# The lead of self and cross attention: four maxima products side by side in PSUM and one reduction for the four

## What is computed

```python
h1 = _ln(x, n1_g, n1_b)
x = _attn(h1, h1, q1, k1, v1, o1_w, o1_b, heads) + x        # self, 20 heads of 16, 512 keys
h2 = _ln(x, n2_g, n2_b)
x = _attn(h2, context, q2, k2, v2, o2_w, o2_b, heads) + x   # cross, 20 heads of 16, 1024 keys
...
sim = jnp.einsum('bhid,bhjd->bhij', q, k) * scale
a = jax.nn.softmax(sim, axis=-1)
```

## Time and profile before

| | us |
|---|---|
| median of three runs | 925.62 |
| the profiled execution | 928.74 |
| its span, first to last instruction | 926.9 |
| TensorE busy in the span | 851.4 |
| VectorE busy in the span | 615.8 |
| ScalarE busy in the span | 470.8 |
| mean granted TensorE clock | 0.936 of full speed |

### The profile page before, as it was taken

How to read it: one execution, slowest core, us unless ns; L and a number is a source line. 1 busy time by engine, 2 the same in 40 slices (tenths; PEclk the granted TensorE clock), 3 DMA queues, 4 the chain that set the end, 5 groups by cost and what they waited for, 6 DMA issues and landing times.

```text
span 926.9 us, 11358 instructions
## 1 busy us (share of the span) xinstructions
PE 851.4 (92%) x4148; PEld 465.4 (50%) x4148; DVE 615.8 (66%) x1156; ACT 470.8 (51%) x682; POOL 82.1 (9%) x109
## 2 busy tenths in 40 slices
PE   4769989999999999999999789999999999799998
PEld 3646744444466576333334433333333332478988
DVE  4245547777683555799966587899999991756132
ACT  4523444445552441466675403667777679465030
POOL 3200000400004021000000300000000000130000
PEclk9977999999997998599999955999999999989999
DMA  6938668632302065122216230222222000600000
GB/s 219 273 113 238 195 179 261 179 97 85 101 19 65 0 197 175 48 68 68 62 28 111 74 108 1 53 53 53 53 52 53 1 2 2 240 1 1 29 1 29
DMA packets 30966, 83.18 MB, mean 90 GB/s; under 512 B 5172, under 2 KB 9212, under 8 KB 28606
## 3 DMA queue, kind: packets, MB, share of 16 engines
q1 hardware_dynamic: 30110, 79.71, 30.4%
q0 software_dynamic: 800, 2.73, 1.0%
HBM read 56.12 MB, written 25.89 MB: 88 GB/s over the span
## 4 chain that ended last, share of the span: by engine, by line
PE 60%; DVE 25%; DMA 7%; ACT 4%; issue 3%; POOL 1%; SPq 0%; DVEq 0%; ACTq 0%; POOLq 0%
PE PS L859 16%; PE PS L802 13%; DVE maxp L961 10%; PE PS L1390 8%; PE PS L553 8%; PE PS L839 6%; DVE negm L961 5%; PE PS L1402 4%; DMA k_d<-split 2%; DMA q_sl<-msplit 2%; PE PS L1200 2%; DMA ca_nat<-in_ca 2%; DVE turned L994 1%; ACT probs L925 1%; DVE stats L1243 1%
## 5 line engine op out<-in xcount | busy, mean ns | idle before, releaser
L925 ACT ACTIVATE probs<-PS 128x1024 f32<-128x1024 f32 (+1 forms) x336 | 311.7, 971 | 153.0 <-PE PS L839 147.4
L961 DVE TENSOR_REDUCE maxp<-PS 128x1 f32<-128x512 f32 x448 | 280.1, 679 | 49.9 <-PE PS L802 48.9
L802 PE MATMUL PS<-k_sl,q_sl 48*128 48x512 f32 (+3 forms) x640 | 264.1, 493 | 23.5 <-DMA q_sl<-q_d 11.1
L802 PEld LDWEIGHTS PS<-k_sl,q_sl 48*128 48x128 f32 (+2 forms) x640 | 120.2, 201 | 201.1 <-DVE maxp L961 121.2
L839 PE MATMUL PS<-q_sl,k_sl 50*128 50x512 f32 (+3 forms) x672 | 204.2, 434 | 9.4 <-ACT probs L925 5.2
L961 DVE TENSOR_REDUCE negm<-PS 128x1 f32<-128x512 f32 (+1 forms) x192 | 120.9, 679 | 28.1 <-PE PS L802 28.0
L839 PEld LDWEIGHTS PS<-q_sl,k_sl 50*128 50x128 f32 (+2 forms) x672 | 103.3, 192 | 57.2 <-ACT probs L925 24.6
L859 PE MATMUL PS<-probs,v2c 128*32 128x512 f32 x640 | 88.3, 622 | 1.0
L591 DVE TENSOR_TENSOR split<-PS,split 128x512 fp32r<-128x512 f32 (+3 forms) x54 | 34.9, 650 | 48.7 <-ACT split L568 48.5
L859 PE MATMUL PS<-probs,v0c 128*64 128x512 f32 (+1 forms) x256 | 62.9, 612 | 0.0
L568 ACT CAST split<-PS 128x512 fp32r<-128x512 f32 (+3 forms) x54 | 29.9, 553 | 56.0 <-PE PS L553 46.5
(11 more groups left out here) (180 smaller groups left out, 1005.4 us busy)
## 6 DMA issues: line engine op xcount, KB each, us to landing
k_d<-split SPq DMA_DIRECT2D x20, 512.0 KB, 3.5
q_d<-split SPq DMA_DIRECT2D x12, 512.0 KB, 3.2
k_sl<-k_d SPq DMA_DIRECT2D x8, 640.0 KB
k_sl<-k_d SPq DMA_DIRECT2D x40, 128.0 KB
q_sl<-q_d SPq DMA_DIRECT2D x40, 128.0 KB
k_sl<-k_d SPq DMA_DIRECT2D x20, 256.0 KB
w_raw<-in_ff_w SPq DMA_DIRECT2D x1, 3840.0 KB, 11.7
k_d<-split SPq DMA_DIRECT2D x10, 256.0 KB, 3.7
```

Of the source, the lines that this page charges most:

```text
L802: nc.tensor.matmul(PS[0:a.qt, SBANKS[k % 3], 0:cn], q_view(g)[f:f + a.rows, j // a.stack, q * a.qt:(q + 1) * a.qt], k_view(g)[f:f + a.rows ...
L925: nc.scalar.activation(probs[0:a.size[t], x % PRING, :, 0:a.nq], PS[0:a.size[t], 2 * (x % 2):2 * (x % 2) + 2, 0:a.nq], ACT.Exp, scale=a.sc ...
L961: nc.vector.tensor_reduce((maxp if nch > 1 else negm)[0:a.qt, g.turn, o:o + 1], PS[0:a.qt, SBANKS[k % 3], 0:a.chunks[c][1]], AX.X, ALU.max ...
```

## The change

In a stream whose first group has `stack` 2 (self and cross attention) the lead is written anew; the steps behind it and the first block's attentions stay.

- TensorE (`wide_items`): the four items of chunk c go to four neighbouring banks, 0 to 3 for even c and 4 to 7 for odd c. From chunk 2 on TensorE waits, once for each chunk, until the chunk that had these banks is reduced.
- VectorE (`wide_maxima`): one reduction reads the four banks, 128 x 2048 elements, and writes four columns. It waits for all four items and adds 4 to `score_free` at its end.
- The flip in the lead takes the last bank of the set that the next chunk uses (`flip_bank`). It waits until the chunk ahead of its own is reduced, and the next chunk's fourth item waits for ScalarE's copy of it.
- Behind the lead TensorE waits until all chunks but the last are reduced, since the first scores go to banks 0 to 3.

```diff
+    def wide_bank(c):
+
+        return 4 * (c % 2)
+
+    def flip_bank(st, i):
+
+        at_chunk = st.first_step[i + 1] if i + 1 < len(st.groups) else len(st.steps)
+        if st.groups[0].a.stack == 2 and at_chunk < st.lead:
+            return wide_bank(at_chunk + 1) + 3
+        return SBANKS[st.flip_use[i] % 3]
+
     def pe_attention(pe, st, side=None):
+        wide = st.groups[0].a.stack == 2
+
+        def wide_items(c):
+            per = st.groups[0].a.per_step
+            if c >= 2:
+                pe.wait_ge(st.score_free, per * (c - 1))
+            for n, (i, m) in enumerate(st.chunk(c)[1]):
...
+                if n == 3 and c and st.chunk(c - 1)[0] is not None:
+                    pe.wait_ge(st.flipped, st.chunk(c - 1)[0] + 1)
+                c0, cn = a.chunks[part]
+                f = a.base(j)
+                nc.tensor.matmul(PS[0:a.qt, wide_bank(c) + n, 0:cn],
...
+                                 start=True, stop=True).then_inc(st.score, 1)
+            if st.chunk(c)[0] is not None:
+                pe.wait_ge(st.score_free, per * c)
+                flip(st.chunk(c)[0], waits=False)
...
         for x in range(st.lead):
-            maxima([x])
...
-            flips([x])
+            if wide:
+                wide_items(x)
...
+        if wide:
+            pe.wait_ge(st.score_free, st.groups[0].a.per_step * (st.lead - 1 + st.lead % 2))
...
+        def wide_maxima(c):
+            ended, items = st.chunk(c)
+            if ended is not None:
+                part_maxima(ended)
...
+            dve.wait_ge(st.score, st.item_at[i, m] + a.per_step)
...
+            nc.vector.tensor_reduce(to, PS[0:a.qt, wide_bank(c):wide_bank(c) + 4, :].rearrange(
+                "p (c e) n -> p c e n", e=a.stack), AX.X, ALU.max,
+                negate=len(a.chunks) == 1).then_inc(st.score_free, a.per_step)
```

More of the change, by code:

```diff
@@ L784, in sp_cross @@
                 sp_load(sp, st, i + SLOTS)
-    def pe_attention(pe, st, side=None):
+    def wide_bank(c):
[5 more added lines that the diff above has]
+        return SBANKS[st.flip_use[i] % 3]
+    def pe_attention(pe, st, side=None):
+        wide = st.groups[0].a.stack == 2
[4 more added lines that the diff above has]
+            for n, (i, m) in enumerate(st.chunk(c)[1]):
+                g = st.groups[i]
+                a = g.a
+                j, q, part = a.items[m]
+                if m == 0:
+                    pe.wait_ge(q_loaded[g.place], g.loads)
+                if n == 3 and c and st.chunk(c - 1)[0] is not None:
[3 more added lines that the diff above has]
+                nc.tensor.matmul(PS[0:a.qt, wide_bank(c) + n, 0:cn],
+                                 q_view(g)[f:f + a.rows, j // a.stack, q * a.qt:(q + 1) * a.qt],
+                                 k_view(g)[f:f + a.rows, j // a.stack, c0:c0 + cn],
+                                 start=True, stop=True).then_inc(st.score, 1)
+            if st.chunk(c)[0] is not None:
+                pe.wait_ge(st.score_free, per * c)
+                flip(st.chunk(c)[0], waits=False)
         def bank_free(k):
@@ L805, in item, with flip @@
                              start=True, stop=True).then_inc(st.score, 1)
-        def flip(i):
+        def flip(i, waits=True):
             g = st.groups[i]
             a = g.a
-            k = st.flip_use[i]
             pe.wait_ge(st.m_low, i + 1)
-            bank_free(k)
-            nc.tensor.transpose(PS[0:2 * a.cols, SBANKS[k % 3], 0:a.qt],
+            if waits:
+                bank_free(st.flip_use[i])
+            nc.tensor.transpose(PS[0:2 * a.cols, flip_bank(st, i), 0:a.qt],
                                 mparts[0:a.qt, g.turn, 0:2 * a.cols].bitcast(F32),
@@ L865, in pe_attention @@
         for x in range(st.lead):
-            maxima([x])
-            if side is not None:
-                pe_projection(pe, side, share(side, x, st.lead))
-            flips([x])
+            if wide:
+                wide_items(x)
+            else:
+                maxima([x])
+                if side is not None:
+                    pe_projection(pe, side, share(side, x, st.lead))
+                flips([x])
+        if wide:
+            pe.wait_ge(st.score_free, st.groups[0].a.per_step * (st.lead - 1 + st.lead % 2))
         if side is not None:
@@ L909, in flipped @@
                     nc.scalar.copy(msplit[0:2 * a.cols, g.turn, 0:a.qt],
-                                   PS[0:2 * a.cols, SBANKS[st.flip_use[i] % 3], 0:a.qt]).then_inc(st.flipped, 1)
+                                   PS[0:2 * a.cols, flip_bank(st, i), 0:a.qt]).then_inc(st.flipped, 1)
         for c in range(st.lead):
@@ L963, in reduce @@
                                     AX.X, ALU.max, negate=nch == 1).then_inc(st.score_free, 1)
+        def wide_maxima(c):
+            ended, items = st.chunk(c)
+            if ended is not None:
+                part_maxima(ended)
+            i, m = items[0]
+            g = st.groups[i]
+            a = g.a
+            t = m // a.per_step
+            dve.wait_ge(st.score, st.item_at[i, m] + a.per_step)
+            if len(a.chunks) > 1:
+                to = maxp[0:a.qt, g.turn, :].rearrange("p (e r c) -> p r c e", e=a.stack, c=2)[:, t, :, :]
+            else:
+                to = negm[0:a.qt, g.turn, :].rearrange("p (e r c) -> p r c e", e=a.stack, c=2)[:, t, :, :]
+            nc.vector.tensor_reduce(to, PS[0:a.qt, wide_bank(c):wide_bank(c) + 4, :].rearrange(
+                "p (c e) n -> p c e n", e=a.stack), AX.X, ALU.max,
+                negate=len(a.chunks) == 1).then_inc(st.score_free, a.per_step)
         def maxima(chunks, normalising=None):
@@ L1008, in dve_attention @@
         for x in range(st.lead):
-            maxima([x])
-            if side is not None:
-                dve_projection(dve, side, share(side, x, st.lead))
+            if st.groups[0].a.stack == 2:
+                wide_maxima(x)
+            else:
+                maxima([x])
+                if side is not None:
+                    dve_projection(dve, side, share(side, x, st.lead))
         for s, (i, t) in enumerate(st.steps):
```

## The result

| | before | changed |
|---|---|---|
| median of 22 runs each, us | 927.6 | 924.0 |
| lowest and highest | 922.9, 932.4 | 915.1, 933.1 |
| the profiled execution, us | 928.7 | 915.5 |
| self lead, first item to first scores, us | 18.9 | 16.8 |
| cross lead | 28.7 | 25.8 |

The account below looks back on a forecast made before the run. VectorE was taken to bound both leads. First chunk, wide reductions at 2.17 us, `part_maxima` and hand-over gave 16.5 and 25.8 us, saving 2.4 + 2.8 = 5.2 us: 925.6 - 5.2 = 920.4 us, range 916.0 to 925.5.

Parts of the forecast that it names:

- What bounds the leads: Both attention leads: VectorE's reductions, 0.599 us apart, set the pace and TensorE waits for its banks.
- The pitch, P = 2.17 us: Leads: wide reductions of 2.25 us, overlapping by 0.08 us, start 2.17 us apart; four single ones take 2.40 us.
- The fear that crossing a bank costs something: Rival, wide reductions in the leads: bank or segment costs raise the pitch to 2.40 us; gain 1.1 us, 924.5 us; chance 0.12.
- First chunk: Start of each lead: VectorE waits for four items instead of starting after 0.50 us; 0.73 us self, 1.2 us cross.
- Middle and end of the lead: `part_maxima` takes 0.34 and 0.55 us, flip hidden; first scores wait until 2.2 us of VectorE work remains, not 1.9.
- The sum for the leads: First item to first scores: 16.5 us self, 25.8 us cross; gains of 2.4 and 2.8 us, together 5.2 us.
- The items hide: Leads: TensorE refills four banks in some 1.2 us during a 2.17 us reduction; rival of exposed items 12 us slower, chance 0.04.
- The border: Leads: four items taking longer than 2.17 us from the freeing of their bank set put TensorE's turn onto the path.
- The clock: Rival behind both leads: 1.2 GHz stretches end a step later (923.6 us, chance 0.12) or earlier (917.2 us, chance 0.14).
- The price of 0.38 us a microsecond: Steps behind the leads: each microsecond at 1.2 GHz loses about 0.38 us; the two stretches cost 10.4 us.
- Where nothing stood in the sum: Both leads: they lie wholly on the path, and nothing behind them is bound by an outside time.
- the two signs of being wrong: The prediction is wrong if the leads shorten by less than 3 us together, or steps get slower at the same clock.

Follow-up runs that it names:

- the two-bank reduction: Changed kernel with two VectorE reductions of two banks each in place of one of four; 1.215 us per reduction, leads 17.0 and 26.3 us.
- half-key experiment: Changed kernel whose wide reduction reads 256 of each item's 512 keys; reductions start 1.32 us apart, leads 10.5 and 16.0 us.
- the reordering: Changed kernel with each chunk's four items issued in the order 0, 2, 1, 3; four items take 1.23 us, leads 16.84 and 25.93 us.

## Why the prediction was right

**What bounds the leads.** Right. VectorE sets the pace, before and after: its wide reductions follow each other without a pause but for `part_maxima`, while TensorE is idle for 1 us in each chunk.

**The pitch, P = 2.17 us.** 2.20 us was measured. The step behind it, a line through a 288 ns and a 681 ns reduction with segments and results at nothing, gave 2.25 us for one; it is 2.283. The fear that crossing a bank costs something is unfounded, as the two-bank reduction shows: 1.215 us on the same line. The overlap of 0.08 us between successive reductions is there for wide ones as well. The page of the Trainium skill weighed there (VectorE: DVE Perf Modes, "Side-by-side: where the cycles go for N=2048 bf16") has 2,293 ns for 2048 bf16 elements at one a cycle, and the record says 2,283 for float32. But its rule under "Terms", that an operation issues only when the pipe before it is empty, would give 2.29 us of pitch, and 2.20 was measured: the measurement decides.

**First chunk.** I took 0.73 and 1.2 us to the first reduction; 0.84 and 0.85 us were measured. The second was 0.35 us too long, which hid what eleven pitches at 2.20 instead of 2.17 us add in the cross lead. That this lead came out at 25.8 us to the tenth is luck: two errors cancel.

**Middle and end of the lead.** `part_maxima` and the flip behave as reckoned: 0.34 us between reductions in self attention, ScalarE's copy done 0.8 us behind the parts, and the next chunk's items ready in time. For the end of the lead the sum is right and the sentence on it wrong. It calls starting the scores with more of VectorE's work left "a small loss". But the lead ends with the first scores, so it is a gain: they now start 2.1 us before the last reduction ends, and started 1.6 us before it. The prediction never named this and the stop behind the flip as gains, though the sum holds them: of its 5.2 us, 4.1 are the pitch, less 0.9 for the later first reduction, and some 2.0 are this. Measured, they are 3.6 less 0.7, and 2.2 (four single reductions in the new banks). The sum for the leads was 16.5 and 25.8 us, measured 16.8 and 25.8; the gain 2.4 + 2.8, measured 2.1 + 2.9.

**The items hide.** Right in the result, with 0.7 us to spare (half-key experiment). The border was drawn too late: it was to decide "from 2.17 us on", and products of 2.14 us in a chunk already gave a pitch of 2.29. The freed set has 2.12 us for items and hand-over, so by estimate the border is near 1.9 us. The reason given for their overlap, neighbours in different rows of the array, did not survive the reordering.

**The clock.** That the stretch of low clock behind a lead varies from run to run and not with the change was the point on which the profiled pair could have misled by more than the whole gain, and it came true in the pair itself. The prediction had it from two stretches of different length in one execution. The price of 0.38 us a microsecond was somewhat high for the program as a whole, where the fit over 80 runs gives 0.31. The Trainium skill (TensorE: Matmul & The Clock Gate, "A second HAM failure mode: psum-queue depth-cycling") tells of a kernel whose clock swings because short pauses stand between its groups of products. The trace agrees to this extent: pauses of 1 us between groups of items go with a mean clock of 0.51 in the cross lead. It does not swing there, though. It stays down. And it stays down as well in the kernel with two more products a chunk, where the pauses are some 0.2 us.

**Where nothing stood in the sum.** That both leads lie wholly on the path holds: 5.0 us in the leads of the trace, 5.1 us in the ratio, though its interval (3.2 to 7.0 us) would not show a loss of a microsecond. Of the two signs of being wrong that the prediction named neither came: the leads shortened by more than 3 us, and at 2.4 GHz a step, from the start of one exponential to that of the same pair a step later, takes 2.90 us in self and 2.75 us in cross attention, before and after (mean behind the eighth step).

## What to carry to other kernels

Where a short reduction repeats back to back, price merging by its pitch, not by its length: here four cost 2.40 us by pitch and 2.72 by length, and one in their place 2.20. Nearly half of the gain (2.2 of 5.0 us) came from what the larger buffer set does at the flip and at the end of the stage, so read those places as well as the pace. When two profiled executions differ by more than the medians do, compare the stages that the change cannot reach and the clock of each before crediting the change.

## What the hardware showed that was not expected

- A VectorE reduction that reads four PSUM banks, or four short segments in four banks, costs what its elements cost and one fixed part of 0.15 us: 2.283 us for 4 x 512, 1.22 us for 4 x 256 in four banks, 1.215 us for 2 x 512 in two.
- Four products of 48 rows, two in either set of rows of the array, take 1.22 us at 1.2 GHz when neighbours lie in different rows and 1.23 us when they lie in the same.
- With TensorE given two more full products in every chunk of 2.2 to 2.6 us, its clock stayed at 1.2 GHz through a lead of 28 us. With ten of them without a pause, 4.0 and 4.6 us, it rose at the burst's end in both leads of the one profile. What is enough for it stays open.
